# Two blocks of copies reordered on ScalarE, and the queries' transposes issued before a wait, in a gated delta-rule attention kernel

## The reference

```
mixed = xn @ W            # q, k, v; a causal convolution of 4 taps; silu
z     = xn @ W_z
for each token t:
    S    = S * exp(g[t])
    u    = (v[t] - k[t] @ S) * beta[t]
    S    = S + outer(k[t], u)
    o[t] = q[t] @ S
x += (rmsnorm(o) * w * silu(z)) @ W_out
```

## Time and profile before

| | us |
|---|---|
| median of 3 runs | 4872.94 (4872.4 to 4873.02) |
| the profiled execution, its own time | 4877.72 |
| its span in the trace | 4875.9 |
| PE (TensorE matmul) busy | 4422.5 (91%) |
| DVE (VectorE) busy | 3851.4 (79%) |
| ACT (ScalarE) busy | 3001.7 (62%) |
| POOL (GpSimd) busy | 985.9 (20%) |

### The profile page before, as it was taken

The page is one execution under the profiler, slowest core; times in us unless marked ns, Lnnn a source line. Parts: engine busy times, 40 slices in busy tenths (PEclk is TensorE's granted clock), DMA queues, the critical chain, the costliest instruction groups (busy, mean ns, idle before and its releaser), DMA issues. The chain is left out here.

```text
span 4875.9 us, 93464 instructions
## 1 busy us (share of the span) xinstructions
PE 4422.5 (91%) x32596; PEld 3629.1 (74%) x32596; DVE 3851.4 (79%) x8126; ACT 3001.7 (62%) x9834; POOL 985.9 (20%) x1252
## 2 busy tenths in 40 slices
PE   4999938999999999999959998499999999999998
PEld 3578827888888888888845876387888888888887
DVE  6938988888888888888841699788888888888886
ACT  1146626777777777777711665467666767676665
POOL 0024311221212121212200443012121212121211
PEclk7899969999999999999979999699999999999999
DMA  1036642222222222222210566222222222222222
GB/s 55 30 90 174 187 137 68 81 75 81 82 77 77 76 83 76 81 78 82 62 31 13 156 187 181 81 77 81 72 80 73 80 76 81 76 82 71 79 74 64
DMA packets 580413, 422.56 MB, mean 87 GB/s; under 512 B 392808, under 2 KB 476312, under 8 KB 579502
## 3 DMA queue, kind: packets, MB, share of 16 engines
q1 hardware_dynamic: 563566, 408.20, 28.6%
q0 software_dynamic: 16384, 8.42, 1.0%
HBM read 296.24 MB, written 120.16 MB: 85 GB/s over the span
## 5 line engine op out<-in xcount | busy, mean ns | idle before, releaser
L1221 DVE SCALAR_TENSOR_TENSOR conv_l<-mix_l,taps_l,conv_l 128x512 f32<-128x512 f32 x1152 | 865.1, 751 | 269.3 <-ACT conv_l L1048 241.8
L854 PE MATMUL pj_l<-x_high,w_high_l 128*128 128x512 f32 x1280 | 588.4, 460 | 160.2 <-ACT w_high_l L1057 160.2
L1423 POOL TENSOR_TENSOR fac_l<-den_l,powers 128x4 f32<-128x4 f32 x256 | 258.0, 1008 | 1782.9 <-DVE den_l L1344 1779.1
L854 PE MATMUL pj_l<-x_high,w_low_l 128*128 128x512 f32 x1280 | 521.4, 407 | 42.1 <-DVE W_l L1309 42.1
L854 PE MATMUL pj_l<-x_low,w_high_l 128*128 128x512 f32 x1280 | 513.1, 401 | 0.0
L637 POOL DMA_DIRECT2D own_dram<-key_kkS_l x512 | 293.9, 581 | 924.7 <-ACT key_kkS_l L509 914.5
L1022 PE MATMUL gb_l<-wo_l,gT_l 128*128 128x256 f32 x2048 | 478.6, 384 | 0.0
L1189 ACT ACTIVATE Z_l<-gb_l 128x128 f32<-128x128 f32 x1024 | 267.7, 289 | 307.3 <-PE gb_l L1013 307.3
L1022 PEld LDWEIGHTS gb_l<-wo_l,gT_l 128*128 128x128 f32 x2048 | 372.6, 190 | 67.7 <-ACT Z_l L1189 24.3
L1354 DVE SCALAR_TENSOR_TENSOR x<-gb_l,fac_l,x 128x256 f32<-128x256 f32 x1024 | 413.0, 476 | 9.0
L854 PEld LDWEIGHTS pj_l<-x_high,w_high_l 128*128 128x128 f32 x1280 | 241.9, 189 | 230.8 <-ACT w_high_l L1057 160.5
(11 more groups left out here) (204 smaller groups left out, 10655.9 us busy)
## 6 DMA issues: line engine op xcount, KB each, us to landing
rows_l<-rows_dram SPq DMA_DIRECT2D x128, 1024.0 KB, 5.6
k_dram<-kT_l SPq DMA_DIRECT2D x128, 256.0 KB, 2.4
kk_dram<-key_kkS_l SPq DMA_DIRECT2D x128, 256.0 KB, 2.4
kq_l<-k_dram SPq DMA_DIRECT2D x128, 256.0 KB, 3.4
kkS_l<-kk_dram SPq DMA_DIRECT2D x128, 256.0 KB, 5.8
w_raw_l<-in_wx SPq DMA_DIRECT2D x32, 640.0 KB
lane_k_l<-own_dram SPq DMA_DIRECT2D x32, 512.0 KB, 4.1
t_dram<-lane_t_l SPq DMA_DIRECT2D x14, 1024.0 KB, 4.9
```

The source lines that it names most:

```text
L854: ins = nc.tensor.matmul(pj_bank(c, t), wt[:, k, t, :], xt[:, k, :, at], start=(k == 0 and n == 0), stop=(k == KD - 1 and n == 2))
L1221: ins = nc.vector.scalar_tensor_tensor(out, mix[:, t, :, i:i + P], wt(i), out, ALU.mult, ALU.add)
L1423: nc.gpsimd.tensor_tensor(fac[:, g, :], den[:, g, :], m.powers[:, 1, :], ALU.pow).then_inc(fac_ok[g], 1)
```

## The change

On TensorE the queries' transposes go ahead of the waits for `x_in`, `x_cp` and `z_cp`; they keep their own two waits (`q_silu`, `vn_ok`). On ScalarE `copy_mix` of projection 2 goes behind `copy_right` and both `copy_z`, and in slots with c > 0 `copy_corner` goes ahead of `square_queries`; with c = 0 it stays behind. No instruction is added or removed.

```diff
@@ body of TensorE @@
                     fill(3)
+                    if not last:
+                        queries_token_major(nh, ncn, False)
                     pe.wait_ge(x_in, 32 * (it + 1))
                     pe.wait_ge(x_cp, 4 * it + 1)
                     for g in range(GROUPS):
                         pe.wait_ge(z_cp[g], it + 1)
-                    if not last:
-                        queries_token_major(nh, ncn, False)
                     for b in range(BATCH):
@@ body of ScalarE @@
                         silu_conv(nh, ncn, 0)
+                    copy_right(it)
+                    for g in range(GROUPS):
+                        copy_z(g, it)
+                    if not last:
                         copy_mix(nh, ncn, 2, False)
-                    copy_right(it)
-                    for g in range(GROUPS):
-                        copy_z(g, it)
                     copy_left(it)
                     if c == 2 and h < KHEADS - 1:
                         for t in range(CONVS):
                             split_weights(h + 1, t)
                     if not last:
                         silu_z(nh, ncn, 0)
+                    if c > 0:
+                        copy_corner(it)
+                    if not last:
                         square_queries(nh, ncn)
-                    copy_corner(it)
+                    if c == 0:
+                        copy_corner(it)
                     if not last:
                         silu_z(nh, ncn, 1)
```

More of the change, by code:

```diff
@@ L1158, in body @@
                         silu_conv(nh, ncn, 0)
-                        copy_mix(nh, ncn, 2, False)
                     copy_right(it)
@@ L1162, in body @@
                         copy_z(g, it)
+                    if not last:
+                        copy_mix(nh, ncn, 2, False)
                     copy_left(it)
```

## The result

The changed kernel takes **4908.41 us** (median of 4 runs, 4903.56 to 4912.82); the kernel before took 4872.83 beside it (4 runs, 4872.4 to 4873.02). The ratio is 1.0069 [1.0053, 1.0085]: 35.6 us slower, where 20.1 were forecast.

The account below looks back on a forecast made before the run. TensorE was nearly gapless, but VectorE's late results often set its pace. Terms +15.5, +11.1, -3.4, -5.0, +6.7 and -4.8 sum to +20.1 us on 4872.9: 4893.0 us, own range 4883 to 4906, 8-in-10 range 4861 to 4913.

Parts of the forecast that it names:

- TensorE 0.42 sooner at L876, stall gone: TensorE, queries' transposes: they start 0.42 us sooner without the stall, a gain only where TensorE then decides.
- Convolution 2 late by 0.19 to 0.20: VectorE, every slot: mix 2 behind the Z copies makes convolution 2 start 0.19 to 0.20 us late.
- Squares end 1.02 later, `query_columns` 0.74 late, VectorE idle for 0.46 ahead of it: ScalarE and VectorE, c = 1: squares behind the corner end at 999.73, so query_columns can't start before 999.76.
- L1326 could start 1.20 later: VectorE's right-hand side, c = 1: starts 1.20 us after the diagonals' start, at 1001.03 instead of 1000.67, net delay 0.36.
- the pace of ScalarE's copies: ScalarE: how closely copies follow in new places, at best 0.16 us overlap, at worst 0.03 behind plus some 0.1.
- Layer 0, c = 0, gain 0.21 and some 0.1 for the squares' wait inside L1022: TensorE at L1022: start 0.21 us sooner (-3.4 us over 16 slots); squares' wait goes in c = 0 to 2 (-4.8 us).
- In layer 0 L1022 begins on a wait for the gate: TensorE, layer 0: a sign expected in the changed profile, L1022 starting on a wait for VectorE's gate.
- TensorE's wait at L967 is gone: TensorE at L967: the wait for the corner copy, 31.0 us in c = 2, vanishes; L967 comes 0.77 us sooner there.
- Layer 1's L1013 grows by 0.42 + 0.36: TensorE, layer 1, c = 1: the wait for VectorE's gate grows by TensorE's gain, 0.42, plus VectorE's delay, 0.36.
- The first (squares not last): Rival: squares end by 999.18, so query_columns starts behind the convolution; sum -17.7 us, 4855 us; chance 0.11.
- The second (a uniform overlap of 0.09): Rival: ScalarE's copies overlap wherever they follow each other, squares end at 999.54; sum +1.8 us, 4875 us; chance 0.16.
- The third (waits cost more: 0.25 on the squares): Rival: fresh waits of the Z and corner copies put the squares 0.25 us later; 23.5 us more, 4916 us; chance 0.12.

Follow-up runs that it names:

- kernel 1: Kernel before with only the queries' transposes moved ahead of TensorE's waits, ScalarE's order unchanged: 4863.44 us, ratio 0.9973.
- Kernel 3: Changed kernel with copy_mix of projection 2 back ahead of copy_right, corner still ahead of the squares: 4895.56 us, ratio 1.0039 to the kernel before.
- kernel 4: Kernel before with only the corner copy moved ahead of the squares for c > 0, transposes not moved: 4926.27 us, ratio 1.0104.
- kernel 6: Changed kernel with the squares in a tile of their own and query_columns behind the right-hand side: 4864.42 us, ratio 0.9978 to the kernel before.
- kernel 7: Changed kernel with copy_mix 2 back in place, squares in their own tile, query_columns behind the right-hand side, c = 2 weight splits later: 4804.60 us, ratio 0.9855.

## Why the forecast was right in kind and short in size

The 4908.4 us lie inside the range for 8 in 10 (4861 to 4913), near its upper end, and outside the forecast's own range (4883 to 4906). The way was called with a chance of 0.66, and by the path that the runs show; the loss was 1.8 times the forecast one.

By its own steps, slot c = 1 of layer 0:

- *TensorE 0.42 sooner at L876, stall gone:* 0.40, no idle time. Right; alone it brings 15 us (kernel 1).
- *Convolution 2 late by 0.19 to 0.20:* 0.17 (997.28 - 988.83 = 8.45 against 8.28). Right.
- *Squares end 1.02 later, `query_columns` 0.74 late, VectorE idle for 0.46 ahead of it:* 1.01, 0.74 (11.25 against 10.51), 0.46. Right. Kernel 3 shows that the corner alone makes this delay when c > 0.
- *The step that was sized too small: "L1326 could start 1.20 later [...] at 1001.03, in place of 1000.67 (1.20 is two steps of 0.60; the row's 1.28 has an overlap of 0.08)".* The forecast let the right-hand side start 0.08 before the diagonals are over, as the operations ahead of it do. It starts 0.04 behind their end: 1001.48 - 1000.15 = **1.33**, in the change and in kernels 3 (1000.25 - 998.92) and 4 (1003.99 - 1002.66), and 1.32 in kernels 6 and 7. In the kernel before, the wait for L967 covered this step, so no row showed it for this pair. The prediction called the pace of ScalarE's copies the one size not read from a row; that size held, and this one, which it took over from another pair of operations, did not. So the net delay is 0.49 in place of 0.36. With c > 0 there are 94 such slots in both layers: 94 x 0.13 = 12.2 of the 14.1 us by which the slots' +34.2 exceeds the forecast's 20.1. In c = 2 the delay was 13.57 - 12.98 = 0.59 for a forecast of 0.42 (1029.35 - 1016.37 in the earlier trace rows, and 1029.98 - 1016.41 in the change). The 0.04 beyond the same 0.13 is there already at `query_columns`: 12.17 from the slot's start, where the forecast's squares allow 12.13 (1028.47 + 0.03 - 1016.37).
- *Layer 0, c = 0, gain 0.21 and some 0.1 for the squares' wait inside L1022:* 0.23 in all, which is 16 x 0.08 = 1.3 us short. The 0.1 was nearly right: the stretch from L1022 to the slot's end is 0.09 to 0.10 shorter in c = 0, 1 and 2. The 0.21 was too much: L1022 starts 0.14 sooner (18.99 from the slot's start, before 19.13). The gate's first half ends where the forecast put it (982.91 + 0.68 = 983.59, in the next fence), but L1022 follows 0.15 behind, not 0.05. Only in c = 0 does L1022 stand behind a wait for the output weights (`wo_ok`) as well; whether that is the reason wasn't tried.

```profile
982.91 1.28 DVE L1301 TENSOR_TENSOR gT_l<-zT_l,gb_l 128x512 f32<-128x512 f32 x2
983.74 3.74 PE L1022 MATMUL gb_l<-wo_l,gT_l 128*128 128x256 f32 x16
```

- *"In layer 0 L1022 begins on a wait for the gate":* it does, but the wait is short. In c = 1 the gate's first half ends at 22.47 from the slot's start and L1022 starts at 22.52, after 0.12 us without a weight load. What the forecast didn't have is a wait just ahead of it: the second group of L1013 waits for the state (`s_ok`, L1293), 0.23 us in c = 1 and 0.61 in c = 2. VectorE makes the state right before the gate, so both waits pass on the same delay.
- *"TensorE's wait at L967 is gone":* not in c = 2. L967 starts 0.76 sooner there (forecast 0.77), but still 21.5 us of waiting for the corner stand in the table. It cost nothing: in c = 2 VectorE is held by the squares, as the next fence shows (slot starts at 1016.41).

DVE and PE of the change, c = 2:

```profile
1028.58 0.17 DVE L1246 TENSOR_SCALAR qcol_l<-ss_kq_l 128x4 f32<-128x4 f32 x1 [0.38 <-ACT diag_b_l L1076]
1028.65 1.29 DVE L1254 TENSOR_TENSOR diag_b_l<-eye,bcol_l 128x512 f32<-128x512 f32 x2
1029.98 2.16 DVE L1331 SCALAR_TENSOR_TENSOR vn_l<-gb_l,run_columns_l,vn_l 128x128 f32<-128x128 f32 x8
```

```profile
1027.43 2.05 PE L967 MATMUL gb_l<-S_l,kq_l 128*128 128x128 f32 x16 [0.21 <-ACT X_l L1141]
```

- *Layer 1's L1013 grows by 0.42 + 0.36:* in a slot with c = 1 the second group's wait for the gate is 0.98 in place of 0.20, that is 0.78 more: right for this row, though the slot itself grew by 0.47. PE's rows in the kernel before (slot starts at 3374.44) and then in the change (slot starts at 3378.05):

```profile
3397.07 0.66 PE L1013 MATMUL gb_l<-eye,gT_l 128*128 128x128 f32 x4 [0.20 <-DVE gT_l L1296]
```

```profile
3401.17 0.66 PE L1013 MATMUL gb_l<-eye,gT_l 128*128 128x128 f32 x4 [0.98 <-DVE gT_l L1301]
```

*The rivals.* The first (squares not last) is refuted by the 0.46 us of idle time. The second (a uniform overlap of 0.09) wanted the squares to end at 999.54 - 988.51 = 11.03; they end at 11.21. The Z copies end at 996.05 and mix 2 starts at 996.07; the corner ends at 998.87 and the squares start at 998.90. Across a change of the first partition nothing overlaps, and the new order has three such pairs. So the Trainium skill's sentence on back-to-back ACTIVATEs (ScalarE: Activation LUTs, What ACT_TABLE_LOAD costs), some 93 ns of overlap, holds here for `silu_z` behind `copy_left` and not across partition ranges; the measurement decides. The third (waits cost more: 0.25 on the squares) is refuted by the squares' end. Its time of 4916 is not far from the 4908 measured, but by another mechanism: the squares are where the forecast had them, and what is dearer is the step behind.

## What to carry to other kernels

Before work is moved ahead of something on an engine with idle time, look up who waits for what is pushed back, and how much reserve it has: here 0.31 us of reserve was spent on a corner copy whose gain on TensorE was lost, since VectorE's gate was what TensorE waited for next. Where an order suffers from a wait for a shared scratch tile, give the tile away first (kernel 6: the same order, some 45 us less) and then reorder. And a step between two operations can only be read where nothing waits between them. Where a wait covers it in the profile, look at which rows (partitions) each operation reads and writes, and take the step from a pair that changes them in the same way.

## What the runs showed of the hardware that was not expected

- VectorE's operations mostly follow each other with 0.08 us of overlap, but the right-hand side starts 0.03 to 0.04 behind the end of the diagonals, in five kernels alike. The kernel before had steps of this kind elsewhere:

```profile
1005.65 0.86 DVE L1272 TENSOR_TENSOR corner_a_l<-kkS_l,decay_l 64x256 f32<-64x256 f32 x2
1006.54 1.29 DVE L1276 TENSOR_TENSOR ap_l<-kk_l,decay_l 128x512 f32<-128x512 f32 x2
1007.75 2.15 DVE L1288 SCALAR_TENSOR_TENSOR S_l<-S_l,rows_l,gb_l 128x128 f32<-128x128 f32 x8
```

  L1276 starts 0.03 behind the end of L1272; L1288 starts 0.08 ahead of the end of L1276. L1288 reads PSUM and stands behind a wait of its own, as the right-hand side does, so neither of these makes the step by itself. What fits the pairs of this slot is the partition at which they begin. The last operation to read PSUM ahead of the right-hand side is the fourth W update (L1309), which begins at partition 64, while the right-hand side begins at 0. The second L1272 writes from partition 64 on, and L1276 from 0 on. The four W updates begin at 32, 0, 96 and 64, and none overlaps the one ahead (0.03 behind, in both traces). From L1276 to L1288 nothing changes. (Where an operation needs the result of the one ahead, as between the passes of a convolution, it is 0.03 to 0.04 behind as well.) No run changed the partitions, so this is a reading of the traces and not shown by a test.
- ScalarE's copies of this chain overlap by 0.09 to 0.16 us where their first partition is the same, and by nothing, 0.02 to 0.03 behind, where it changes. This held for each new pair that the changed order made. It is the partition read from that counts: the two corner copies of a slot write from the same one and read from 0 and from 64, and the second starts 0.02 behind the first, in every slot.
- The stretch between the layers differs by up to 10 us between the ten traces (689 to 699 us), and a group of 64 matmuls in it takes from 7.36 us, at a granted clock of 1.00, to 13.9. Each kernel was profiled once, so the traces don't show whether executions of one kernel differ in this too. For a change of this size two profiled spans are too coarse a comparison; the slots' own lengths are not.
